# Routing as a pipeline over four batches, the last batch's row scatters moved into the expert block, and tile fields read eight at a time

## The chip, the core and the metric

The kernel runs on one core of a Trainium2 chip. The metric is the device time of one execution in microseconds (us); the engines are TensorE (PE), VectorE (DVE), ScalarE (ACT), GpSimd (POOL) and SyncE (SP). SP and POOL issue the DMAs.

## What is computed

The input is `x` (4 batches of 512 tokens with 512 channels) and a context. Four residual steps follow one another: a cross attention, a feed-forward layer whose weights come from spline control points, a selective scan, and a mixture of experts. Only the last two steps touch the change:

```python
x = x + _L1_xattn_ref(ctx_1024, _layernorm(x), ...)      # y * silu(z), z = layernorm(x)
x = x + _L1_ffn_ref(_layernorm(x), gate_kernel, gate_proj, up_proj, down_proj)

router_logits = x2d @ gate_kernel                        # 2048 tokens, 32 experts
routing_weights, selected = top_k(softmax(router_logits), 8)
routing_weights = routing_weights / sum(routing_weights)
inter = silu(rows_of_expert @ gate_proj[e]) * (rows_of_expert @ up_proj[e])   # 512 -> 192
output[token] += routing_weight * (inter @ down_proj[e])                      # 192 -> 512
```

## The kernel before, in words

The program is a row of blocks; at the end of a block every engine waits for all others. Blocks A and B (attention, feed-forward, scan) end at about 1055 us of the trace and are not touched.

**Block C** (`block_c`, L750) finishes the scan step and routes. It goes over the four batches one after the other; a batch is 4 tiles of 128 tokens. For each batch DVE normalizes `z` (L390), ACT takes its silu (L958), DVE multiplies with `y` (L854), PE turns the product (L976), DVE adds it to `X` (L858) and takes the statistics of the new `X` (L862 to L872), writes the normalized rows into `C_row` (L876), PE turns them (L981), ACT copies them (L963) and PE makes the router's logits (L986, 16 small matmuls, two records each). DVE then does softmax and top 8 (L882 to L900), PE counts the places of the rows in each expert's region (L991 to L995), and DVE writes the 32 destination rows of each partition into `C_where` (L909). POOL then issues 32 scatters (L829), one for each tile and each of a token's 8 experts; each writes 128 rows of 2180 bytes (512 channels, 32 weights, the token's number) into `rows_d` in HBM. Two row buffers alternate. After the fourth batch DVE computes 168 entries of tile fields in the tensor `meta` (L933 to L951): for each tile of 128 rows its expert, its first row, its weight slot and flags. SP appends to each of the 32 experts' regions a tile of padding (L810 to L813), and waits for all of them before the block ends.

**Block D** (`block_d`, L1007) computes the experts. SP loads the weights of experts 0 and 1 (L1045, L1046) and the first 8 row tiles (L1051), ACT and POOL split the weights in high and low parts (L1142, L1143; L1197, L1198). A loop then takes 8 tiles in one turn (`UNROLL`). For each tile PE turns the inner product of the tile (L1114), does gate and up of the next tile (12 matmuls, `split_products`, L1087 to L1089), turns the rows of the tile after that (L1083) and does the down product (6 matmuls). DVE copies the result (L1192) and POOL adds it into the output with an indirect DMA (L1218). SP refills the row buffer once the tile's addition has landed (L1070, L1071). At each expert's first tile SP loads the weights of the expert three further on, ACT and POOL split those of the expert two further on.

The engines read a tile's fields with `field` (L1036), one `value_load` of one word: PE three for each tile (its slot, the next slot, the next expert), ACT one flag for each tile and three more where it splits, POOL two flags and three more, SP one flag and a base, and two more where it loads weights.

Of the kernel before, what the change touches and what calls it, by code (L numbers as in the profile page):

```python
# [39 lines left out]
ROW = D + NE + 1  # L40
REGION = NB * L + P
# [52 lines left out]
def build(nc, a):  # L94
# [9 lines left out]
    with ctx:  # L104
# [12 lines left out]
        block_c(nc, a, X, ident, bank, meta, y0_d, y1_d, rows_d)  # L117
        block_d(nc, a, ident, bank, meta, rows_d)
# [631 lines left out]
def block_c(nc, a, X, ident, bank, meta, y0_d, y1_d, rows_d):  # L750

    with ExitStack() as s:
        sb, sem = mem(nc, s, "C")
        st, mv, rstd = sb("st", [P, NT, 6]), sb("mv", [P, NT, 2]), sb("rstd", [P, NT])
        st2, mv2, rstd2 = sb("st2", [P, LT, 6]), sb("mv2", [P, LT, 2]), sb("rstd2", [P, LT])
        y = [sb(f"y{i}", [P, LT, L]) for i in range(2)]
        z, yg = sb("z", [P, LT, D]), sb("yg", [P, LT, L])  # L760
        gk, hT = sb("gk", [P, KC, NE]), sb("hT", [P, LT, D])
        row = [sb(f"row{i}", [P, LT, ROW]) for i in range(2)]
        tok = sb("tok", [P, NT], I32)
        before, ones = sb("before", [P, P]), sb("ones", [P, P])
        lg, ex, pr, rest, chosen, place = (sb(n, [P, LT, NE]) for n in ("logit", "expo", "prob", "rest", "chosen", "place"))
        mx, sm, inv, tsum, tinv = (sb(n, [P, LT]) for n in ("mx", "sm", "inv", "tsum", "tinv"))
        top, top_place = sb("top", [P, LT, TOPK]), sb("top_place", [P, LT, TOPK])
        where = [sb(f"where{i}", [P, LT, TOPK], I32) for i in range(2)]
        fill = sb("fill", [P, NE])
        pad = sb("pad", [P, ROW])  # L770
        incl, neg_base, tau, tau0 = sb("incl", [NE, NE]), sb("neg_base", [NE, 1]), sb("tau", [NE, NMETA]), sb("tau0", [1, NMETA])
        need_i, need_s, need, ends = sb("need_i", [NE, 1], I32), sb("need_s", [NE, 1], I32), sb("need", [NE, 1]), sb("ends", [NE, 1])
        past = sb("past", [NE, NMETA])
        ev, sc, dd, f0, f1 = (sb(n, [1, NMETA]) for n in ("ev", "sc", "dd", "f0", "f1"))
        i0, i1 = sb("i0", [1, NMETA], I32), sb("i1", [1, NMETA], I32)
        padrow = sb("padrow", [1, NE], I32)

        stats, root, ln_step, ln_var, ln_rooted = sem("stats"), sem("root"), sem("ln_step"), sem("ln_var"), sem("ln_rooted")
        ld_y, joined, ld_c = [sem(f"ld_y{i}") for i in range(2)], [sem(f"joined{i}") for i in range(2)], sem("ld_c")
        z_in, z_done, g_done, yT_ps, x2_done, h_in, h_ps, h_sb, lg_ps = (sem(n) for n in ("z_in", "z_done", "g_done", "yT_ps", "x2_done", "h_in", "h_ps", "h_sb", "lg_ps"))  # L780
        passed = sem("passed")
        r_step, r_in, r_exp, chosen_done, rank_ps, where_done, scattered, fill_done = (
            sem(n) for n in ("r_step", "r_in", "r_exp", "chosen_done", "rank_ps", "where_done", "scattered", "fill_done"))
        fT_ps, need_done, ends_ps, past_done, meta_ps, m_step, padrow_done, stored = (
            sem(n) for n in ("fT_ps", "need_done", "ends_ps", "past_done", "meta_ps", "m_step", "padrow_done", "stored"))
        block = s.enter_context(nc.Block())
        RS = 15
        out = a["out"]
        consts = ((gk[:, :, :], "gk"), (tok[:, :], "tok"), (before[:, :], "before"), (ones[:, :], "ones"), (fill[:, :], "fill"),
                  (pad[:, 0:ROW - 1], "pad"), (pad[:, ROW - 1:ROW].bitcast(I32), "pad_tok"), (incl[:, :], "incl"),  # L790
                  (neg_base[:, :], "neg_base"), (tau[:, :], "tau"), (tau0[:, :], "tau0"))

        @block.sync
        def _(sp):
            for b in range(2):
                sp.dma_start(y[b][:, :, :], y0_d[b]).then_inc(ld_y[b], 16)
            for dst, name in consts:
                sp.dma_start(dst, a[name]).then_inc(ld_c, 16)
            sp.wait_ge(ld_c, 16 * len(consts))

            sp.dma_start(rows_d[NE * REGION:NE * REGION + P, :], pad[:, :]).then_inc(stored, 16)
            sp.dma_start(out[NT * P:NT * P + P, :], pad[:, 0:D]).then_inc(stored, 16)
            for b in range(NB):
                if b + 2 < NB:
                    sp.wait_ge(g_done, b + 1)
                    sp.dma_start(y[b % 2][:, :, :], y0_d[b + 2]).then_inc(ld_y[b % 2], 16)
                sp.wait_ge(x2_done, 4 * b + 4)
                sp.dma_start(out[b * L:(b + 1) * L, :].rearrange("(t p) n -> p t n", p=P), X[:, b * LT:(b + 1) * LT, :]).then_inc(stored, 16)
# [5 lines left out]
            sp.wait_ge(stored, 16 * (2 + NB + NE))  # L814

        @block.gpsimd
        def _(g):
            def join(b):

                g.wait_ge(ld_y[b % 2], 16 * (b // 2) + 16)  # L820
                g.dma_start(y[b % 2][:, :, :], y1_d[b], accum_op=ALU.add).then_inc(joined[b % 2], 16)

            join(0)
            join(1)
            for b in range(NB):
                g.wait_ge(where_done, b + 1)
                for t in range(LT):
                    for k in range(TOPK):
                        g.indirect_dma_start(rows_d[:, :], bass.IndirectOffsetOnAxis(ap=where[b % 2][:, t, k:k + 1].bitcast(U32), axis=0),  # L829
                                             row[b % 2][:, t, :], None).then_inc(scattered, 16)  # L830
                if b + 2 < NB:
                    join(b + 2)
                g.wait_ge(scattered, (b + 1) * 16 * LT * TOPK)

        @block.vector
        def _(v):
            ln_statistics(v, X, st, mv, rstd, stats, root, 0)
            v.wait_ge(ld_c, 16 * len(consts))
# [4 lines left out]
            def batch(base, h):  # L843
                def step(i, n):
                    i.then_inc(r_step, 1)
                    v.wait_ge(r_step, base * RS + n)
                    if n in (4, 5, 13):
                        v.sem_inc(passed)
                for t in range(LT):
                    i = ln_tile(v, X, base * LT + t, mv, rstd, z[:, t, :])  # L850
                i.then_inc(z_in, 1)
                v.wait_ge(z_done, base + 1)
                v.wait_ge(joined[h], pair * 16 + 16)
                v.tensor_tensor(yg[:, :, :], y[h][:, :, :], z[:, :, :], ALU.mult).then_inc(g_done, 1)  # L854
                for t in range(LT):
                    v.wait_ge(yT_ps, base * 4 + t + 1)
                    x = X[:, ds(base * LT + t, 1), :].rearrange("p o n -> p (o n)")
                    v.tensor_tensor(x, bank[t][:, :], x, ALU.add).then_inc(x2_done, 1)  # L858
                v.wait_ge(x2_done, base * 4 + 4)
                v.sem_inc(passed)  # L860
                for t in range(LT):
                    i = v.bn_stats(st2[:, t, :], X[:, ds(base * LT + t, 1), :])  # L862
                i.then_inc(ln_step, 1)
                v.wait_ge(ln_step, base * 3 + 1)
                v.sem_inc(passed)
                for t in range(LT):
                    i = v.bn_aggr(mv2[:, t, :], st2[:, t, :])
                i.then_inc(ln_step, 1)
                v.wait_ge(ln_step, base * 3 + 2)
                v.tensor_scalar(rstd2[:, :], mv2[:, :, 1], EPS, None, ALU.add).then_inc(ln_var, 1)  # L870
                v.wait_ge(ln_rooted, base + 1)
                v.reciprocal(rstd2[:, :], rstd2[:, :]).then_inc(ln_step, 1)  # L872
                v.wait_ge(ln_step, base * 3 + 3)
                v.wait_ge(scattered, pair * ((1 + h) * 16 * LT * TOPK))
                for t in range(LT):
                    v.tensor_scalar(row[h][:, t, 0:D], X[:, ds(base * LT + t, 1), :].rearrange("p o n -> p (o n)"), mv2[:, t, 0:1],  # L876
                                    rstd2[:, t:t + 1], ALU.subtract, ALU.mult).then_inc(h_in, 1)
                v.tensor_copy(row[h][:, :, ROW - 1:ROW].bitcast(I32), tok[:, ds(base * LT, LT)].rearrange("p (t o) -> p t o", o=1))

# [9 lines left out]
                for t in range(LT):  # L889
                    i = v.max(top[:, t, :], pr[:, t, :])  # L890
# [22 lines left out]
            with v.Fori(0, NB // 2) as pair:  # L913
                for h in range(2):
                    batch(pair * 2 + h, h)
# [361 lines left out]
```

## Time and profile before

| what | value |
|---|---|
| median of 3 runs | 2109.48 us (2105.89 to 2111.84) |
| profiled execution, its own time | 2110.38 us |
| its span, first to last instruction | 2108.6 us |
| busy share of the span | PE 78%, DVE 51%, ACT 36%, POOL 58% |
| block C | 1055 to 1339 us |
| block D | 1339 us to the end, 144 tiles |

The span is the time from the first to the last recorded instruction. Busy time counts work of the engines' data paths only; reading a register from memory, a branch or a wait is not busy time, and shows as "issue" where nothing else explains that an engine stood idle. Where a row says "remote", the engine was released by an event that no record of this core explains.

### The profile page before, as it was taken

What the parts mean: (1) busy time and instruction counts of PE and PEld (TensorE: products, weight loads), DVE (VectorE), ACT (ScalarE), POOL (GpSimd) and SP (SyncE); (2) the same over time, 40 slices, a digit from 0 to 9 for tenths busy, and PEclk for the clock granted to TensorE, in tenths of its full rate; (3) what the DMA queues carried; (4) which work ended last, traced back from release to release, by engine and by line L of the source; (5) the groups of instructions that cost most, each with busy time, mean ns of one, the idle gap of its engine ahead of it and who ended that gap; (6) DMA issues with size and microseconds to landing.
All of it is one profiled execution on the core that took longest, in us unless ns stands there. A gap on an engine that the chain in (4) does not pass through costs nothing. (4 is left out here: it accounts for less than half of the span.)

```text
span 2108.6 us, 28900 instructions
## 1 busy us (share of the span) xinstructions
PE 1643.6 (78%) x6083; PEld 1036.1 (49%) x6084; DVE 1070.7 (51%) x1770; ACT 762.8 (36%) x1072; POOL 1225.3 (58%) x552
## 2 busy tenths in 40 slices
PE   5887577989899999999933221299888998988886
PEld 2333233444344444444433221277777777777775
DVE  3566665555656565656552331054554544544453
ACT  3434345555555555555421110132222322232221
POOL 0111239888888888889715665256555545655552
PEclk9888779999999999999955555599999999999998
DMA  3111325668576767767656647667777877877776
GB/s 110 71 70 71 149 93 147 146 129 194 125 140 153 166 130 140 164 132 138 120 156 214 209 189 252 218 123 163 159 162 151 161 146 165 168 160 161 146 141 114
DMA packets 100442, 313.48 MB, mean 149 GB/s; under 512 B 13633, under 2 KB 14562, under 8 KB 88530
## 3 DMA queue, kind: packets, MB, share of 16 engines
q0 software_dynamic: 40896, 144.79, 35.9%
q1 hardware_dynamic: 59410, 167.42, 26.5%
q14 instruction: 117, 0.96, 0.2%
q8 instruction: 19, 0.31, 0.1%
HBM read 145.08 MB, written 167.08 MB: 148 GB/s over the span
## 5 line engine op out<-in xcount | busy, mean ns | idle before, releaser
L684 DVE TENSOR_TENSOR_SCAN B_E<-bank,B_E 128x512 f32<-128x512 f32 x256 | 306.4, 1212 | 206.7 <-ACT bank L639 199.2
L1218 POOL DMA_INDIRECT out_x<-D_y,D_rows x144 | 223.0, 1549 | 293.2 <-issue 177.8
L727 POOL TENSOR_TENSOR B_E<-B_E,B_Cb 128x2048 f32<-128x2048 f32 x64 | 291.8, 4559 | 110.9 <-DVE B_E L684 110.9
L721 POOL TENSOR_TENSOR B_E<-B_dtu,B_Bb 128x2048 f32<-128x2048 f32 x64 | 292.1, 4565 | 33.2 <-DMA B_Bb<-bc_d 33.2
L600 PE MATMUL bank<-B_Wd,B_inter 128*128 128x512 f32 x512 | 230.7, 596 | 33.2 <-DVE X L678 32.4
L590 PE MATMUL bank<-hT,B_Wg 128*128 128x512 f32 x512 | 236.8, 606 | 23.5 <-DVE B_inter L673 22.4
L590 PE MATMUL bank<-hT,B_Wu 128*128 128x512 f32 x512 | 230.2, 592 | 0.0
L1087 PE MATMUL bank<-D_gu_hi,D_xT_hi 128*128 x580 | 215.1, 371 | 15.5 <-DVE D_xT_lo L1176 8.3
L639 ACT ACTIVATE bank<-B_dtv,negA 128x512 f32<-128x512 f32 x256 | 171.8, 687 | 137.8 <-DVE B_E L684 137.0
L1171 DVE SCALAR_TENSOR_TENSOR D_inner<-D_sil,D_rows,bank 128x192 f32<-128x192 f32 x145 | 60.1, 414 | 308.4 <-ACT D_sil L1139 300.0
L1139 ACT ACTIVATE D_sil<-bank 128x192 f32<-128x192 f32 x145 | 47.2, 326 | 427.8 <-PE bank L1089 424.4
L1089 PE MATMUL bank<-D_gu_hi,D_xT_lo 128*128 x580 | 200.3, 345 | 0.0
L1088 PE MATMUL bank<-D_gu_lo,D_xT_hi 128*128 x580 | 200.0, 345 | 0.0
L829 POOL DMA_INDIRECT rows_d<-C_row,C_where x128 | 129.7, 1013 | 118.1 <-DVE C_where L909 80.3
L600 PEld LDWEIGHTS bank<-B_Wd,B_inter 128*128 128x128 f32 x512 | 92.7, 189 | 155.7 <-issue 92.0
L590 PEld LDWEIGHTS bank<-hT,B_Wg 128*128 128x128 f32 x512 | 97.3, 194 | 144.6 <-issue 142.8
L1197 POOL TENSOR_TENSOR D_gu_lo<-D_raw_gu,D_gu_hi (+1 forms) x32 | 111.2, 3474 | 81.9 <-issue 41.9
L590 PEld LDWEIGHTS bank<-hT,B_Wu 128*128 128x128 f32 x512 | 97.3, 190 | 122.5 <-issue 122.5
L1176 DVE TENSOR_TENSOR D_xT_lo<-bank,D_xT_hi 128x512 fp32r<-128x512 f32 x146 | 101.0, 692 | 88.9 <-ACT D_xT_hi L1135 88.0
L1083 PE MATMUL bank<-ident,D_rows 128*128 128x128 f32 x584 | 89.9, 277 | 71.4 <-DMA D_rows<-rows_d 71.4
L1087 PEld LDWEIGHTS bank<-D_gu_hi,D_xT_hi 128*128 128x128 f32 x580 | 112.8, 194 | 43.5 <-issue 36.9
L1087 PE MATMUL bank<-D_d_hi,D_iT_hi 96*128 x288 | 125.9, 437 | 0.0
(205 smaller groups left out, 2713.1 us busy)
## 6 DMA issues: line engine op xcount, KB each, us to landing
y_d<-B_E POOLq DMA_DIRECT2D x64, 1024.0 KB, 8.0
D_rows<-rows_d SPq DMA_DIRECT2D x152, 272.5 KB
D_raw_gu<-in_wgu SPq DMA_DIRECT2D x32, 768.0 KB
B_Bb<-bc_d SPq DMA_DIRECT2D x32, 512.0 KB, 5.4
B_Cb<-bc_d SPq DMA_DIRECT2D x32, 512.0 KB, 4.0
D_raw_d<-in_wd SPq DMA_DIRECT2D x32, 384.0 KB
rows_d<-C_pad SPq DMA_DIRECT2D x33, 272.5 KB
X<-in_x SPq DMA_DIRECT2D x4, 1024.0 KB, 9.1
```

Source lines behind the costliest of these rows:

```text
L590: mm = pe.matmul(ps[:, :], W[:, k, ch * P:(ch + 1) * P], hT[:, k, tb * L:(tb + 1) * L], start=k == 0, stop=k == KC - 1)
L600: mm = pe.matmul(Yb[t % 2][:, :], inter[jj % 2][:, ch, t * P:(t + 1) * P], Wd[w][:, ch, :], start=ch == 0, stop=ch == 1)
L639: act.activation(dA[m % 2][:, :], dtv[:, c, :], ACT.Exp, scale=negA[:, c, n:n + 1]).then_inc(dA_done, 1)
L684: v.tensor_tensor_scan(E[:, s % NR, c, :], dA[m % 2][:, :], E[:, s % NR, c, :], 0.0, ALU.mult, ALU.add).then_inc(s_done, 1)
L721: g.tensor_tensor(E[:, s % NR, :, :], dtu[b % 2][:, :, :], spread(Bb[jj % 2][:, s % 2, :]), ALU.mult).then_inc(dbu_done, 1)
L727: g.tensor_tensor(E[:, s % NR, :, :], E[:, s % NR, :, :], spread(Cb[jj % 2][:, s % 2, :]), ALU.mult).then_inc(prod_done, 1)
L829: g.indirect_dma_start(rows_d[:, :], bass.IndirectOffsetOnAxis(ap=where[b % 2][:, t, k:k + 1].bitcast(U32), axis=0), row[b % 2][:, t, :], ...
L1087: pe.matmul(ps, hi, whi, start=n == 0, stop=False)
L1088: pe.matmul(ps, hi, wlo, start=False, stop=False)
L1089: return pe.matmul(ps, lo, whi, start=False, stop=last)
L1197: g.tensor_tensor(slot(gu_lo, buf), slot(raw_gu, raw), slot(gu_hi, buf), ALU.subtract)
L1218: g.indirect_dma_start(a["out"], bass.IndirectOffsetOnAxis(ap=rows[i][:, ROW - 1:ROW].bitcast(U32), axis=0), ysb[i][:, :], None, compute_o ...
```

## The change

- `X` normalization and silu become one ACT activation for each tile, with a scale and a shift (`silu`); the rows are normalized by ACT too (`rows`). DVE keeps the statistics, additions and routing.
- The batches are interleaved: each engine has an order written out by hand (`gate`, `residual`, `normal`, `route`, `choose`, `rank` on DVE). There is a row buffer for every batch, so no batch waits for the scatters of another. The ranks come from 2 matmuls of 128 columns for each batch instead of 14 of 32.
- The weights of experts 0 and 1 are loaded and split in block C (class `Weights`), in POOL's queue ahead of the first scatter.
- Block C scatters batches 0 to 2 only and pads experts 0 to 15. Block D begins with the 32 scatters of batch 3, the lowest of each token's experts first; SP loads row tile `i` when the scatters of the first `i + 1` places have landed, then the weights of expert 2, then pads experts 16 to 31, waits for these, and enters the loop.
- In the loop PE reads nine slots and nine experts in one `load` each at the head of 8 tiles, and ACT its eight split flags; the ring positions are computed from the expert's number instead of being read.
- The result tiles use the space of `X`.

```diff
-FIELDS = 11
-BASE, EXPERT, SLOT, FIRST, LOADS, SPLITS, LOAD_RAW, SPLIT_RAW, SPLIT_SLOT, GO, RLOADS = range(FIELDS)
+FIELDS = 8
+BASE, EXPERT, SLOT, FIRST, LOADS, SPLITS, GO, RLOADS = range(FIELDS)
# block C, POOL
+            join(2)
+            join(3)
+            split(0)
+            split(1)
+            for b in range(NB - 1):
+                scatter(b)
# block C, DVE
+            gate(0)
+            gate(1)
+            residual(0)
+            residual(1)
+            gate(2)
+            normal(0)
+            residual(2)
+            normal(1)
+            v.wait_ge(ld_c, 16 * len(consts))
+            route(0)
+            gate(3)
+            choose(0)
+            residual(3)
+            normal(2)
+            rank(0)
+            route(1)
+            choose(1)
+            normal(3)
+            rank(1)
...
# block C, ACT
+            def silu(b):
+                if b >= 2:
+                    act.wait_ge(yT_ps, 4 * (b - 1))
+                for t in range(LT):
+                    q = LT * b + t
+                    act.activation(z[b % 2][:, t, :], X[:, q, :], ACT.Silu, bias=shift[:, q:q + 1], scale=rstd[:, q:q + 1]).then_inc(z_done, 1)
...
+            split(0)
+            sqrt(2)
+            expo(0)
+            rows(1)
+            hidden(1)
+            sqrt(3)
+            split(1)
...
# block C, SP
-            for e in range(NE):
-                first = sp.value_load(padrow[0:1, e:e + 1], min_val=e * REGION, max_val=(e + 1) * REGION - P)
-                sp.dma_start(rows_d[ds(first, P), :], pad[:, :]).then_inc(stored, 16)
+            for e in range(PADS_FIRST):
+                W.pad(sp, e, rows_d, pad, padrow).then_inc(stored, 16)
# block D
+        def fields(eng, regs, f, tile, hi):
+
+            eng.load(regs, meta[0:1, f, ds(tile, len(regs))])
+            return [eng.snap(r, min_val=0, max_val=hi) for r in regs]
# block D, SP
+            sp.wait_ge(scattered, 16 * (NT - LT) * TOPK)
             for i in range(UNROLL):
                 first = field(sp, BASE, i, NE * REGION)
+                sp.wait_ge(late[TOPK - 1 - i], 16 * LT)
                 sp.dma_start(rows[i][:, :], rows_d[ds(first, P), :]).then_inc(ld_rows[i], 16)
+            W.load(sp, 2, 0)
+            for e in range(PADS_FIRST, NE):
+                W.pad(sp, e, rows_d, pad, padrow).then_inc(padded, 16)
+            sp.wait_ge(padded, 16 * (NE - PADS_FIRST))
# block D, PE
+                    bufs = fields(pe, slots, SLOT, q * UNROLL, NSLOT - 1)
+                    of = fields(pe, experts, EXPERT, q * UNROLL, NE - 1)
                     for i in range(UNROLL):
                         t = q * UNROLL + i
-                        buf, next_buf = field(pe, SLOT, t, NSLOT - 1), field(pe, SLOT, t + 1, NSLOT - 1)
-                        next_expert = field(pe, EXPERT, t + 1, NE - 1)
# block D, POOL
+            for k in reversed(range(TOPK)):
+                for t in range(LT):
+                    g.indirect_dma_start(rows_d[:, :], bass.IndirectOffsetOnAxis(ap=where[:, NT - LT + t, k:k + 1].bitcast(U32), axis=0),
+                                         rows_last[:, t, :], None).then_inc(late[k], 16)
```

## Rows read from the trace of the kernel before

**Rows 1.** Windows over both blocks: stretch, length, busy of each engine, clock, DMA share.
```profile
1055.00:1101.00 46.00, 17.09 (x92) 16.42 (x92) 27.98 (x85) 11.44 (x13) 1.76 (x2) 0.58 0.54 161
1101.00:1159.00 58.00, 20.20 (x92) 19.53 (x92) 18.14 (x59) 8.66 (x10) 33.59 (x33) 0.50 0.63 209
1273.00:1339.00 66.00, 1.93 (x7) 0.60 (x7) 7.79 (x30) 0.00 (x0) 31.09 (x32) 0.50 0.78 271
1395.00:2109.00 714.00, 625.76 (x3297) 525.12 (x3295) 350.43 (x688) 191.25 (x334) 383.93 (x197) 0.97 0.75 154
```

**Rows 2.** Timeline of DVE in block C: start, length, line, idle before.
```profile
1071.45 2.29 DVE L854 TENSOR_TENSOR C_yg<-C_y,C_z 128x2048 f32<-128x2048 f32 x1 [2.08 <-ACT C_z L958]
1074.94 0.69 DVE L858 TENSOR_TENSOR X<-bank,X 128x512 f32 x1 [1.20 <-PE bank L976]
1082.15 1.92 DVE L876 TENSOR_SCALAR C_row<-X,C_mv,C_rstd 128x512 f32 x4
1090.03 0.29 DVE L882 TENSOR_REDUCE C_mx<-bank 128x4 f32<-128x128 f32 x1 [5.88 <-PE bank L986]
1101.30 0.18 DVE L909 TENSOR_SCALAR C_where<-C_top_place 128x32 int32<-128x32 f32 x1
1147.44 0.29 DVE L882 TENSOR_REDUCE C_mx<-bank 128x4 f32<-128x128 f32 x1 [28.60 <-remote]
```

**Rows 3.** POOL in block C: the scatters in 1150 to 1500 us grouped, then its timeline.
```profile
L829 POOL DMA_INDIRECT rows_d<-C_row,C_where x96 | 97.1, 1012 | 71.3 <-DVE C_where L909 43.0 <-issue 28.3
...
1159.69 1.01 POOL L829 DMA_INDIRECT rows_d<-C_row,C_where  x1 [14.86 <-DVE C_where L909]
1313.26 0.97 POOL L829 DMA_INDIRECT rows_d<-C_row,C_where  x1 [0.30 <-issue]
```

**Rows 4.** Timeline of PE in block C, second batch: the logits.
```profile
1120.77 6.88 PE L986 MATMUL bank<-C_gk,C_hT 128*128 128x32 f32 x32
```

**Rows 5.** Timeline of SP's queue: the padding during the scatters, and after them.
```profile
1274.49 39.23 SPq L813 DMA_DIRECT2D rows_d<-C_pad  x15
...
1318.62 17.49 SPq L813 DMA_DIRECT2D rows_d<-C_pad  x17
```

**Rows 6.** Timeline of PE at the start of block D: turned rows of tiles 0 and 8, first product.
```profile
1345.78 1.12 PE L1083 MATMUL bank<-ident,D_rows 128*128 128x128 f32 x4 [69.30 <-DMA D_rows<-rows_d]
1353.44 0.68 PE L1087 MATMUL bank<-D_gu_hi,D_xT_hi 128*128 x1 [6.55 <-POOL D_d_lo L1198]
1394.71 0.60 PE L1083 MATMUL bank<-ident,D_rows 128*128 128x128 f32 x4
```

**Rows 7.** Timelines of SP's queue and POOL, start of block D.
```profile
1340.54 8.07 SPq L1051 DMA_DIRECT2D D_rows<-rows_d  x8
...
1347.59 3.41 POOL L1197 TENSOR_TENSOR D_gu_lo<-D_raw_gu,D_gu_hi 128x1536 fp32r<-128x1536 f32 x1 [33.36 <-ACT D_d_hi L1143]
1350.97 2.33 POOL L1198 TENSOR_TENSOR D_d_lo<-D_raw_d,D_d_hi 96x1024 fp32r<-96x1024 f32 x1
```

**Rows 8.** DMA issues in 1055 to 1101 us: size and median time to landing.
```profile
C_y<-y_d POOLq DMA_DIRECT2D x2, 1024.0 KB, 11.6
```

**Rows 9.** Groups of PE in 1395 to 2109 us: busy, mean ns, idle before and its releaser.
```profile
L1087 PE MATMUL bank<-D_gu_hi,D_xT_hi 128*128 x556 | 205.0, 369 | 8.2 <-DVE D_xT_lo L1176 7.5 <-issue 0.4
L1114 PE MATMUL bank<-ident,D_inner 128*96 128x128 f32 x278 | 57.3, 288 | 60.1 <-issue 41.8 <-DVE D_inner L1171 17.6
```

**Rows 10.** Timeline of PE at the head of one turn of 8 tiles.
```profile
1524.26 0.42 PE L1114 MATMUL bank<-ident,D_inner 128*96 128x128 f32 x2 [1.57 <-issue]
```

**Rows 11.** Chain of waits in 1890 to 1900 us: POOL reads one field after another.
```profile
1896.53 0.29 POOLq L1036
...
1897.22 0.29 POOLq L1036
```

**Rows 12.** POOL: its additions on the page, and its waits for results in 1450 to 2030 us.
```profile
L1218 POOL DMA_INDIRECT out_x<-D_y,D_rows x144 | 223.0, 1549 | 293.2 <-issue 177.8
...
POOL out_x L1218 <- DVE D_y L1192: 42.2, 9, 7.3
```

More of the change, by code:

```diff
@@ L40 @@
 ROW = D + NE + 1
+GUW, MH = 2 * M, M // 2
+PADS_FIRST = NE // 2
 REGION = NB * L + P
@@ new lines, in _ @@
+            i.then_inc(stats, 1)
+            v.wait_ge(stats, 1)
+            for t in range(NT):
+                i = v.bn_aggr(mv[:, t, :], st[:, t, :])
+            i.then_inc(stats, 1)
+            v.wait_ge(stats, 2)
+            v.tensor_scalar(rstd[:, :], mv[:, :, 1], EPS, None, ALU.add).then_inc(stats, 1)
+            v.wait_ge(root, 1)
+            v.reciprocal(rstd[:, :], rstd[:, :]).then_inc(stats, 1)
+            v.wait_ge(stats, 4)
+            v.scalar_tensor_tensor(out=shift[:, :], in0=mv[:, :, 0], scalar=-1.0, in1=rstd[:, :], op0=ALU.mult, op1=ALU.mult).then_inc(shifted, 1)
@@ L906, in batch @@
                 for t in range(LT):
                     i = v.max(top_place[:, t, :], place[:, t, :])
-                step(i, 14)
-                v.tensor_scalar(where[h][:, :, :], top_place[:, :, :], -1.0, None, ALU.add).then_inc(where_done, 1)
-                step(v.tensor_tensor(fill[:, :], bank[2][:, 0:NE], fill[:, :], ALU.add), 15)
-                v.sem_inc(fill_done)
-            with v.Fori(0, NB // 2) as pair:
-                for h in range(2):
-                    batch(pair * 2 + h, h)
@@ new lines, in _ @@
+            route(0)
[8 more added lines that the diff above has]
+            rank(1)
+            route(2)
+            choose(2)
+            rank(2)
+            route(3)
+            choose(3)
+            rank(3)
+            v.tensor_scalar(padrow[:, :], fills[0:1, NT, :], -1.0, None, ALU.add).then_inc(padrow_done, 1)
+            step(v.tensor_tensor(count[:, :], fills[:, NT, :], fills[:, 0, :], ALU.subtract))
@@ new lines, in logits @@
+            def logits(b):
+                for t in range(LT):
+                    pe.wait_ge(row_done, LT * b + t + 1)
+                    if LT * b + t >= 2:
+                        pe.wait_ge(h_sb, LT * b + t - 1)
+                    for k in range(KC):
+                        mm = pe.transpose(bank[4 + t % 2][:, k * P:(k + 1) * P], row[b][:, t, k * P:(k + 1) * P], ident[:, :])
+                    mm.then_inc(h_ps, 1)
+                if b >= 2:
+                    pe.wait_ge(f_step, 5 * (b - 1))
+                for t in range(LT):
+                    pe.wait_ge(h_sb, LT * b + t + 1)
+                    for k in range(KC):
+                        mm = pe.matmul(bank[6 + b % 2][:, t * NE:(t + 1) * NE], hT[t // 2][:, t % 2, k * P:(k + 1) * P], gk[:, k, :], start=k == 0, stop=k == KC - 1)
+                mm.then_inc(lg_ps, 1)
@@ new lines, in ranks @@
+            def ranks(b):
+                pe.wait_ge(chosen_done, b + 1)
+                rhs = chosen[:, LT * b:LT * b + LT, :].rearrange("p t e -> p (t e)")
+                pe.matmul(bank[6 + b % 2][:, P:2 * P], before[:, :], rhs, start=True, stop=True)
+                pe.matmul(bank[6 + b % 2][:, 2 * P:3 * P], ones[:, :], rhs, start=True, stop=True).then_inc(rank_ps, 1)
+            turn_y(0)
+            turn_y(1)
+            turn_y(2)
+            logits(0)
+            turn_y(3)
+            logits(1)
@@ new lines, in _ @@
+            ranks(0)
+            logits(2)
+            ranks(1)
+            logits(3)
+            ranks(2)
+            ranks(3)
+            pe.wait_ge(ends_done, 1)
+            pe.transpose(bank[0][0:NE, 0:P], ends[:, :], ident[:, :])
+            pe.transpose(bank[1][0:NE, 0:P], need[:, :], ident[:, :]).then_inc(endsT_ps, 1)
+            pe.wait_ge(past_done, 1)
+            pe.matmul(bank[2][0:1, 0:NMETA], ones[0:NE, 0:1], past, start=True, stop=True)
+            pe.matmul(bank[3][0:1, 0:NMETA], need_c[:, :], past, start=True, stop=True).then_inc(meta_ps, 1)
```

476 lines of the change are left out of this document (257 added, 219 removed).

## The prediction

> **What bounds the kernel now.** I read the windows over blocks C and D first, then the timelines of DVE, POOL and SP in C, then the groups and the timeline of PE in D.
>
> In block C (1055 to 1339 us) no engine is busy: in 1101 to 1159 us PE works 20 of 58 us, DVE 18, ACT 9, POOL 34, and DMA stands at 0.63 [rows 1]. The order of work bounds it. Batch 0 needs 46 us until its destinations are written at 1101.30 [rows 2]. Then POOL scatters, and a scatter costs 1.012 us and 0.30 us of issue, 1.31 us together, so 42 us for the 32 of a batch [rows 3]. The next batch should be ready in that time. It isn't: DVE waits 28.60 us for "remote" until 1147.44 [rows 2], and POOL, done at 1159.69 - 14.86 = 1144.83, idles 14.86 us until the next destinations come [rows 3]. PE's last logits matmul is recorded at 1127.65 [rows 4], 20 us before DVE is released, and the release comes 2.6 us after POOL falls silent. So while POOL streams scatters, word between engines comes late. SP shows the same: with scatters running 15 paddings take 39.23 us, 2.62 each; without them 17 take 17.49 us, 1.09 each (the last one without its gap) [rows 5]. The fourth batch's scatters end at 1314.23 [rows 3], the padding at 1336.11 [rows 5], and the expert block starts at 1339.
>
> Block D begins with 14 us of loading and splitting before PE's first product at 1353.44; rows of tile 8 are turned at 1394.71 [rows 6]. After that PE is the bound: in the 714 us from 1395 its clock is at 0.97, the high level, and it is busy 625.76 [rows 1]; its gaps are 60.1 us ahead of the inner transpose (41.8 of them "issue", 17.6 DVE) and 8.2 ahead of the first product [rows 9]. The issue gaps are PE's sequencer reading three fields for each tile.
>
> **Terms.** My clock is the start of tile 8's row transposes, 1394.71 in the old trace: it lies behind all that C and the start of D do, and the loop behind it is the same work. Blocks A and B are untouched.
>
> *Start of C to the first scatter.* POOL's first scatter now stands behind both weight splits, and the second waits for ACT's `split(1)`, which waits for `sqrt(3)`, so for `residual(3)`. DVE's queue up to there: its first `gate` can start as now, at 1071.45; four gates of 2.29 (9.2); four residuals of 6.6 (1074.94 to the reciprocal just ahead of 1082.15, less its 0.4 of waiting for the root; 26.4); one softmax and top 8, the stretch from 1090.03 to 1101.30 without 5 us of waiting for PE and 1.4 of ranks (4.9); small steps 0.8 [rows 2]. Sum 1112.7. The loads of `y` for batches 2 and 3 follow the gates, and their accumulating DMA takes 11.6 us [rows 8]; with expert weights in the same DMA engines I add 5 us: 1117.7. Then ACT's split, an estimate of 2.5 (POOL's pass over the same elements, 3.41 + 2.33, is its upper bound), and POOL's 5.7 [rows 7]: 1126. This is 25 us later than now. Below: 1118, if the joins are not late; above: 1140.
>
> *Scatters of batches 0 to 2.* 96 of 1.31 us = 126 us [rows 3], if POOL never starves. Routing of the other batches needs some 34 us of DVE (three times the 11.3 from 1090.03 to 1101.30 [rows 2]) behind the first scatter in good conditions; the scatters of batch 1 are due 42 us after it, of batch 2 at 84. Even with every step two times slower while POOL streams, it arrives in time. End 1252; the tile fields and 16 paddings (at 2.62 us, 42 us [rows 5]) lie beside it. Block D starts at 1254.5 against 1339. The moved DVE work on ACT (16 silus, 16 row tiles) is beside idle time: ACT works 11 of the first 46 us [rows 1]. Fewer rank matmuls cost nothing and save nothing on the path. Where this cover fails is the second rival.
>
> *Start of D.* The 32 scatters of batch 3 take 42 us, to 1296.5. Tile 0 could start after the first four, but PE's word comes late under the stream, so I count one tile of progress until 1296.5. Then PE needs 7 tiles of 4.6 us (625.76 busy over 136 tiles [rows 1]) to reach tile 8's rows: 1329. SP in the meantime: last row tile issued at 1298, weights of expert 2, 16 paddings at 1.09 = 17.5 us [rows 5] and 2 for landing: 1318; then three fields, the next weights, and the row load (4 us), which lands 5.2 us later, as the first did (1340.54 to 1345.78 [rows 6, 7]): 1327.5. Both come out alike; the later is 1329. So 1394.7 - 1329 = **66 us gained**. POOL starts its additions at 1297, some tiles late. It has slack: in 580 us of steady loop it waited 42.2 us for results [rows 12], and now reads two fields fewer at each split. The splits of expert 2 are due only at tile 9 or so (144 additions [rows 12] over 32 experts).
>
> *The loop.* One field read costs 0.69 us from read to read (1896.53 to 1897.22), 0.29 of it the read itself [rows 11]. PE drops three for each tile. What they hide behind are the six down products, so only the excess shows: 1.57 us at the head of a turn [rows 10], less at other tiles. After: at the 17 heads behind my clock two reads of nine words. From below they cost 2 x 0.69 = 1.4 us; from above 18 x 0.69 = 12.4. No row shows a read of more than one word. I take 3.6 us, near the lower end, because the 0.4 us around a read are address and bounds steps that one read needs once. The three old ones were 2.1, so the head's gap grows from about 1.5 to 3.0: 17 x 3.0 = 51. Of the other gaps (8.2 ahead of the product stays; of the 17.6 for DVE most were ACT's four reads ahead of a split, now one) 15 stay. Total 66 against 68.3 now [rows 9]; with ACT's help I say **5 us gained**. At the lower end 0.8 x 17 + 15 = 29, 40 us gained; at the upper end 11.8 x 17 + 15 = 216, 147 lost.
>
> The Trainium skill ("Runtime: NRT & Kernel Launch", the launch sequence) speaks against this part: a register load costs about 200 ns for each register, even in bulk. By it the 18 words are 3.6 us without what stands around them, and the sum would be some 20 us worse. The rows show 0.29 us for one word and no more.
>
> **Sum.** 2110.4 (the profiled execution, span 2108.6 and 1.8 around it) - 66 - 5 = 2039. The median is 0.9 below this execution: **2038 us**.
>
> **Rivals.**
> 1. *Reads are cheap and tiles overlap the last scatters.* For it: no row says that a further word is dear. Gain in the loop up to 40 instead of 5, and a few us earlier at tile 8: 2110 - 70 - 38 = 2002. Against: three out of three batches show late word under the stream.
> 2. *POOL starves in C.* If the late word holds up routing as now, POOL idles 15 us before each of batches 1 and 2 again [rows 3], and the first scatter may be at 1140: 2038 + 30 to + 44 = 2075. Against: all heavy PE work (the logits of batch 3) is queued before or near the first scatter.
> 3. *Slower than before: nine words cost nine reads.* Place: the head of each turn of 8 tiles on PE. Price: 18 x 0.69 = 12.4 us there, 147 us lost over the loop against 66 gained: 2190. It decides from the point where the 18 words cost 3.6 + 71/17 = 7.8 us, 0.43 us a word. For it: the read itself is 0.29 us; against: the rest of the 0.69 shouldn't repeat.
> 4. *The loop doesn't move at all*, since PE then waits for DVE and ACT: 2043. It is within the forecast's own range.
>
> The Trainium skill ("SBUF — State Buffer", who interferes with whom) says that TensorE and ScalarE never wait on anyone and only VectorE and GpSimd share a port. The 28.60 us and SP's 2.62 against 1.09 us don't fit this [rows 2, 5]. By the rule tiles would run beside the last scatters, and the sum would still be within 2 us, since the padding holds tile 8 until 1327.5.
>
> **Numbers.** Forecast with its own range 2015 to 2060: 0.50. Rival 1: 0.20. Rival 2: 0.15. Rival 3: 0.10. Others, such as the expert block slowed by POOL's late additions: 0.05. The range takes rival 1 and 2 in and leaves the worst of 3 out: 1988 to 2090. A change under 0.3% (6 us) can't be told from none here. Faster 0.88 (forecast, rivals 1 and 2, some of the rest), same 0.02, slower 0.10.
>
> **What would show it.** First scatter near 1126; no gap of POOL over 3 us between the 96 scatters; block D near 1255; row transposes of tile 8 near 1329, released by the row load; in the loop PE's gaps ahead of the inner transpose near 3 us at every eighth tile and small elsewhere. Wrong if the first scatter comes after 1140, if POOL waits for destinations again, or if the gap at the heads is over 8 us.

## The result, and the profile after

| | before | after |
|---|---|---|
| device time, median (range, runs) | 2108.67 us (2105.89 to 2111.84, 4) | 2031.14 us (2028.05 to 2034.64, 4) |
| ratio, 95% interval | | 0.9623 [0.9604, 0.9642] |
| profiled execution, its span | 2110.38, 2108.6 | 2028.05, 2026.0 |
| mean granted clock of PE | 0.894 | 0.902 |
| row transposes of tile 8 start | 1394.71 | 1364.39 |
| from there to the end of the span | 713.9 | 661.6 |

The kernel gained 77.5 us in the medians and 82.6 between the two profiled spans (the new kernel's profiled execution is the fastest of its four). The forecast said 2038, 71 us less: 66 ahead of tile 8 and 5 behind it. Measured are 30.3 ahead of it (1394.71 - 1364.39) and 52.3 behind it (713.9 - 661.6). The total is right for the wrong reasons: both terms are far off, in opposite directions.

The windows of the new kernel by stage (columns as in [rows 1]): from the start of C to the first scatter, the first 64 scatters, POOL's gap, the next 32, the barrier, the 32 late scatters, up to tile 8, and the loop.

```profile
1055.00:1133.00 78.00, 30.18 (x177) 27.47 (x178) 52.95 (x145) 43.19 (x58) 15.71 (x13) 0.60 0.66 202
1133.00:1214.00 81.00, 20.98 (x93) 19.71 (x91) 7.02 (x39) 6.48 (x11) 61.69 (x64) 0.50 0.57 217
1214.00:1226.00 12.00, 0.00 (x0) 0.00 (x0) 2.49 (x13) 0.17 (x1) 0.44 (x1) 0.50 0.06 23
1226.00:1266.00 40.00, 3.11 (x10) 1.38 (x10) 11.69 (x57) 0.14 (x1) 30.32 (x32) 0.50 0.70 265
1266.00:1282.00 16.00, 0.00 (x0) 0.00 (x0) 0.00 (x0) 0.00 (x0) 0.06 (x1) 0.50 0.46 174
1282.00:1322.00 40.00, 12.57 (x44) 10.78 (x44) 2.64 (x5) 2.81 (x4) 30.55 (x32) 0.59 0.74 258
1322.00:1364.00 42.00, 29.96 (x134) 25.70 (x134) 14.98 (x30) 7.65 (x14) 17.43 (x13) 0.78 0.82 228
1364.00:2026.00 662.00, 613.30 (x3298) 528.42 (x3298) 351.68 (x688) 198.35 (x334) 383.87 (x196) 0.98 0.76 165
```

In two stretches that the forecast didn't have hardly any engine works, 28 us together: 12 us in the middle of the scatters and 16 us at the end of block C. POOL's waits in C and at the start of D name them (line, what it waited for, us in total, times, longest); in the old kernel it waited 43.0 us for destinations between the batches [rows 3].

```profile
POOL rows_d L851 <- issue: 28.8, 95, 0.3
POOL rows_d L1363 <- POOLq L760: 16.2, 1, 16.2
POOL rows_d L851 <- DVE where L964: 11.6, 1, 11.6
```

The late word of [rows 2] ("word" is the news, by a semaphore, that another engine is done) is back in another place. On PE's timeline the last rank product of batch 2, the third, is recorded at 1167.64; on DVE's the addition that waits for it starts at 1223.04, 9 us after POOL's last scatter of that stream ended (1213.01 + 0.96).

```profile
1167.64 0.37 PE L1124 MATMUL bank<-C_chosen,C_ones 128*128 128x128 f32 x1 [1.03 <-issue]
```

```profile
1223.04 0.87 DVE L957 TENSOR_TENSOR C_fills<-bank,C_fills 128x32 f32<-128x32 f32 x4 [74.52 <-remote]
```

```profile
1213.01 0.96 POOL L851 DMA_INDIRECT rows_d<-C_row,where  x1 [0.30 <-issue]
1225.56 0.96 POOL L851 DMA_INDIRECT rows_d<-C_row,where  x1 [11.59 <-DVE where L964]
```

SP's queue in the new kernel: the first 16 paddings take 44.74 us, 2.8 each on average. That average mixes two rates: the first seven, beside scatters, cost 5.1 us each (1233.89 to 1269.71), the last eight, behind them, 1.09. The 8 row loads take 37.65 us beside the late scatters (8.07 without, [rows 7]).

```profile
1233.89 44.74 SPq L1168 DMA_DIRECT2D rows_d<-pad  x16
1288.84 37.65 SPq L1215 DMA_DIRECT2D D_rows<-rows_d  x8
```

In the loop (PE's waits from 1364 on) two kinds are left; the waits for DVE, 17.6 and 7.5 us in [rows 9], are gone.

```profile
PE bank L1278 <- issue: 32.9, 17, 2.7
PE bank L1246 <- DMA D_rows<-rows_d: 4.1, 1, 4.1
```

The most telling line is a small one in the page's table of DMA queues, which nobody would read first: packets, MB and share of the instruction queue q14 (its packets bring parts of an engine's program), before and then after.

```profile
q14 instruction: 117, 0.96, 0.2%
```

```profile
q14 instruction: 29, 0.24, 0.0%
```

The old kernel loads 88 packets of 8 KB more. In the 16 turns from 1403.56 to 2053.89 there are 80, 5 a turn; the new kernel has none between 1374 and 2027 us.

### The profile page after: what moved, and what is told of

Same layout as the page of the kernel before. It is cut to its first block and busy times, and to the rows that moved or that the text cites. A ratio compares the mean times of both kernels' runs of the same rounds, so it can differ in the third digit from the quotient of the medians.

```text
span 2026.0 us, 26118 instructions
## 1 busy us (share of the span) xinstructions
PE 1612.5 (80%) x5986; PEld 1022.0 (50%) x5987; DVE 1058.9 (52%) x1748; ACT 779.3 (38%) x1097; POOL 1220.6 (60%) x557
## 5 line engine op out<-in xcount | busy, mean ns | idle before, releaser
L1380 POOL DMA_INDIRECT out_x<-X,D_rows x144 | 224.0, 1556 | 279.2 <-DVE X L1353 129.1
L608 PE MATMUL bank<-B_Wd,B_inter 128*128 128x512 f32 x512 | 230.7, 597 | 33.2 <-DVE X L686 32.4
L1250 PE MATMUL bank<-W_gu_hi,D_xT_hi 128*128 x580 | 216.3, 373 | 3.2 <-DVE D_xT_lo L1337 1.8
L1251 PE MATMUL bank<-W_gu_lo,D_xT_hi 128*128 x580 | 200.5, 346 | 0.0
L1252 PE MATMUL bank<-W_gu_hi,D_xT_lo 128*128 x580 | 200.1, 345 | 0.0
L1250 PEld LDWEIGHTS bank<-W_gu_hi,D_xT_hi 128*128 128x128 f32 x580 | 112.9, 195 | 35.3 <-issue 33.5
L1250 PE MATMUL bank<-W_d_hi,D_iT_hi 96*128 x288 | 127.2, 442 | 0.0
L366 POOL TENSOR_SCALAR A_one<-A_ex 128x2048 f32<-128x2048 f32 x4 | 21.5, 5368 | 169.6 <-ACT A_ex L281 169.6
L1299 ACT ACTIVATE D_xT_hi<-bank 128x512 fp32r<-128x512 f32 x146 | 87.1, 597 | 85.5 <-issue 67.6
```

Of the source, the lines that this page charges most:

```text
L608: mm = pe.matmul(Yb[t % 2][:, :], inter[jj % 2][:, ch, t * P:(t + 1) * P], Wd[w][:, ch, :], start=ch == 0, stop=ch == 1)
L1250: pe.matmul(ps, hi, whi, start=n == 0, stop=False)
L1251: pe.matmul(ps, hi, wlo, start=False, stop=False)
L1252: return pe.matmul(ps, lo, whi, start=False, stop=last)
L1380: g.indirect_dma_start(a["out"], bass.IndirectOffsetOnAxis(ap=rows[i][:, ROW - 1:ROW].bitcast(U32), axis=0), ysb[i], None, compute_op=ALU. ...
```

## Experiments

The diffs show the lines that matter; registers, names and helpers that go with them are left out.

Times are medians of the runs made beside the kernel before on the same chip (its medians there: 2114.5 us for the first four kernels, 2113.3 for the last four), so ratios are compared between the two groups and times within one. "Tile 8" is the start of that tile's row transposes; "loop" is the time from there to the last tile's inner transposes in the profiled execution: 691.4 us before, 641.8 after. Three kernels leave the loop's work as it is in the new one (pe_waits16, last_in_c24, pause8). With the new kernel's, their loops span 641.8 to 647.3 us, and the time that PE's clock stands at 0.50 in them goes with it: 13.7, 17.1, 27.3 and 27.3 us. So a difference of less than 6 us between two loops isn't clear by itself.

| kernel | time | ratio, 95% | loop | q14 packets |
|---|---|---|---|---|
| pe_waits16 | 2031.8 | 0.9606 [0.9575, 0.9638] | 642.4 | 29 |
| new_pe_three_reads | 2039.1 | 0.9637 [0.9605, 0.9669] | 654.6 | 29 |
| new_act_single_flags | 2035.9 | 0.9639 [0.9600, 0.9678] | 645.5 | 29 |
| old_pe_nine_words | 2115.5 | 1.0004 [0.9988, 1.0020] | 688.5 | 117 |
| new_pool_long | 2066.0 | 0.9781 [0.9753, 0.9809] | 672.0 | 117 |
| old_pool_short | 2100.0 | 0.9949 [0.9932, 0.9967] | 680.9 | 29 |
| last_in_c24 | 2038.0 | 0.9649 [0.9616, 0.9682] | 645.2 | 29 |
| pause8 | 2043.6 | 0.9671 [0.9643, 0.9699] | 647.3 | 30 |

### Is it PE's program that is fetched again?

**pe_waits16**

```diff
+                        pe.wait_ge(W.hi_done, 1)
+                        pe.wait_ge(xT_first, 1)
```

> The new kernel with 16 waits more in each turn of 8 tiles on PE (two behind every tile's first-layer products, on semaphores that were passed long ago). They read nothing and stand where PE has 12 products queued. In the trace PE issues 511 instructions in a turn of the new kernel and 595 in one of the old; the old one loads some 8 packets of 8 KB of instructions a turn, the new one none between 1373 and 2027 us. Theory A (the loop gained because PE's turn no longer has to be fetched again): 511 + 16 instructions are over the limit again, the packets are back and the kernel takes 2051 to 2076 us. Theory B (the loop gained because PE reads fewer fields): the waits are hidden, 2031 +- 6 us, no packets.

Measured: 2031.8 us, loop 642.4 (641.8 without the waits), 29 packets. Theory A in this form falls: that PE's turn is 511 instructions with the gain and 595 without it was a coincidence. (The old kernel's packets are 5 a turn, not the 8 of the text above.)

**new_pe_three_reads** (the edit is the old code of PE, in the new kernel)

```diff
-                    bufs = fields(pe, slots, SLOT, q * UNROLL, NSLOT - 1)
-                    of = fields(pe, experts, EXPERT, q * UNROLL, NE - 1)
+                        buf, next_buf = field(pe, SLOT, t, NSLOT - 1), field(pe, SLOT, t + 1, NSLOT - 1)
+                        next_expert = field(pe, EXPERT, t + 1, NE - 1)
```

> The new kernel with PE reading its three fields one by one at every tile, as the old kernel did; everything else is new. Theory A (instruction fetching): PE's turn is near 595 instructions again, packets are back, and the loop loses all of its gain, 45 us or so: 2076. Theory B (the reads' own time): the gaps put down to issue go from 33 to 41 us and the waits for VectorE stay away: 2040.

Measured: 2039.1 us. Its runs (2037.5 to 2043.3) lie above all of pe_waits16 (2027.3 to 2032.9) on the same chip, 7 us apart; the loop of the profiled execution is 12.8 us longer. PE's waits there:

```profile
PE bank L1277 <- issue: 35.2, 43, 2.1
```

Theory B named the time, 2040 us, and that no wait for DVE comes back, but not the gaps: it said 41 us, and there are 43 short waits of 35.2 us for 16 of 32.4 in the same stretch. Many small gaps for a few large ones is nearly an even trade in waiting. Most of the 12.8 us lies in PE's busy time, 621.0 us behind tile 8 for 613.3, with the clock at 0.50 for 23.9 us of it, not 13.7. This profiled execution is also the slowest of its four and the new kernel's the fastest, so 12.8 is more than the 7 us of the medians.

**old_pe_nine_words**

```diff
-                        buf, next_buf = field(pe, SLOT, t, NSLOT - 1), field(pe, SLOT, t + 1, NSLOT - 1)
-                        next_expert = field(pe, EXPERT, t + 1, NE - 1)
+                    bufs = fields(pe, slots, SLOT, q * UNROLL, NSLOT - 1)
+                    of = fields(pe, experts, EXPERT, q * UNROLL, NE - 1)
```

> The old kernel with one change: PE reads nine slots and nine experts at the head of a turn, as the new one does. ScalarE, GpSimd and SyncE read as before, block C is the old one. Theory A (instruction fetching): the whole gain of the loop comes from this, 2109 - 45 = 2064 us, no instruction packets in the steady loop. Theory B (the reads' own time, the rest of the gain from ScalarE's fewer reads): 2109 - 8 = 2101 us.

Measured: no change (1.0004). Both theories miss, A by some 45 us, B by 9. The very edit that looked like the point of the new loop is worth nothing in the old one, because something else held PE up there. Its waits show the shift: the issue gaps fall from 41.3 (in this view) to 34.0 us, the waits for DVE rise from 17.6 to 20.6 and from 7.5 to 9.6, and waits for rows from 2.2 to 4.0.

```profile
PE bank L1124 <- issue: 34.0, 19, 2.8
PE bank L1124 <- DVE D_inner L1181: 20.6, 23, 2.7
PE bank L1096 <- DVE D_xT_lo L1186: 9.6, 24, 0.5
```

**new_act_single_flags**

```diff
-                        with act.If(to_split[i] > 0):
+                        with act.If(field(act, SPLITS, t, 1) > 0):
```

> The new kernel with ScalarE reading its split flag one by one at every tile as before (8 reads a turn for one of eight words). Theory A (PE's instructions alone): no change, 2031 +- 6 us. The rival (the waits of PE for VectorE, 25 us in the old loop, came from ScalarE's reads): up to 25 us more, 2056.

Measured: 2035.9 us, 4 more than pe_waits16 on the same chip (2034.7 to 2045.2 against 2027.3 to 2032.9), the loop 3.7 longer, which alone would not be clear. Its waits are: 5.2 us of waiting for DVE's `xT_lo` are back, and none of the kernels with an unchanged loop has any. ScalarE's flags are a small part.

### Is it POOL's?

**new_pool_long**

```diff
                             split_lo(ring(g, e, SPLIT_AHEAD, NRAW), ring(g, e, SPLIT_AHEAD, NSLOT))
+                            for _ in range(8):
+                                g.wait_ge(W.hi_done, 1)
+                                g.sem_inc(passed)
```

> The new kernel with POOL's loop made longer, not slower: eight passed waits, each with a count, behind every weight split, inside the branch that only every fourth tile or so takes (some 2 a turn). Written out, a turn of POOL is then 337 instructions; it is 273 in the new kernel and 313 in the old. The theory that PE's program was being fetched again fell with the first runs: 16 instructions more on PE brought no packet, nine-word reads in the old kernel took none away, and all kernels on the new base have none, all on the old base 83. Of the 85 packets in the old loop 43 land just ahead of the first addition of a turn on POOL. Theory A (POOL's loop is what is fetched): the 8 KB packets come back in the steady loop and it is as slow as the old one, 30 to 45 us more, 2061 to 2076. Theory B (fetching is a by-product, or is another engine's): none or few packets, 2031 +- 6 us.

Measured: ratio 0.9781 against 0.9623 of the new kernel, the intervals far apart: 0.0158 x 2108.7 = 33 us slower. The packets are back, as many as on the old kernel's page, and the loop is 30.2 us longer. The page's line and then POOL's waits in 1420 to 2000 us of this kernel:

```profile
q14 instruction: 117, 0.96, 0.2%
```

```profile
POOL out_x L1380 <- issue: 171.4, 95, 8.7
POOL out_x L1380 <- DVE X L1353: 40.1, 12, 6.8
```

The same waits in the new kernel:

```profile
POOL out_x L1380 <- DVE X L1353: 107.2, 38, 6.6
POOL out_x L1380 <- issue: 102.0, 79, 6.6
```

In the new kernel POOL waits mostly for results: it has slack. With the longer program 69 us more are "issue", its own sequencer, and it waits for results only 12 times. It runs late; row buffers then come free late, and PE gets waits that it didn't have (its waits from 1395 us on):

```profile
PE bank L1246 <- DMA D_rows<-rows_d: 9.6, 7, 3.5
PE bank L1278 <- DVE D_inner L1332: 7.6, 6, 1.8
```

All PE's waits there are 49.1 us for 32.4, so they make up 17 of the 30 us. The other 13 are PE's busy time behind tile 8, 626.61 us for 613.30. The clock stands at 0.50 for 37.5 us of the loop, not 13.7, in 11 falls for 4; at the 1.3 us that a fall costs below, some 9 us of the 13 (an estimate).

```profile
1365.00:2063.00 698.00, 626.61 (x3298) 537.37 (x3298) 350.79 (x688) 196.06 (x334) 383.69 (x196) 0.96 0.73 157
```

The added waits take 0.69 us at each of 30 splits, 21 us in all, on an engine that waits 107 us for results; that alone is not the 69 us. The records of POOL's sequencer show where the rest is. Behind the branch that ends a turn its next record comes after 3.9 us, behind the one that begins the next after 2.2 (medians), 111 us over the loop, a part of it while a split or an addition still works. In the new kernel the same two steps take 0.19 and 0.13 us.

**old_pool_short**

```diff
-                            raw, buf = field(g, SPLIT_RAW, t, NRAW - 1), field(g, SPLIT_SLOT, t, NSLOT - 1)
+                            raw, buf = ring(g, e, SPLIT_AHEAD, NRAW), ring(g, e, SPLIT_AHEAD, NSLOT)
```

> The old kernel with one change, on POOL alone: the two buffer numbers of a split are worked out from the expert (an addition and a mask each) and no longer read. Written out, POOL's turn falls from 313 to 273 instructions, the new kernel's number. Theory A (POOL's loop was fetched again each turn and that slowed the others): the packets go and the old loop gains 30 to 45 us, 2064 to 2079. Theory B (the time of the reads): 30 splits times two reads of 0.69 us on an engine with slack, 2109 +- 6.

Measured: 0.9949 [0.9932, 0.9967], 11 us faster, and the 88 packets are gone. Two reads less, in a branch taken twice a turn, do this. Behind the branch that ends a turn POOL's sequencer stood still for 4.5 us in the old kernel (median of 16, 3.4 to 8.0, 78 us together); here it is 0.20 us. So POOL's program is what was fetched, shown from both sides. But the 30 to 45 us were not there: PE then still reads three fields a tile, and keeps 33.5 us of issue gaps and 26.4 us of waits for DVE. How the 11 us divide between the fetching and the reads that POOL no longer does (30 times two of 0.69 us, 41 us) is not separated. POOL waited 52.6 us for results in 1420 to 2000 us before, and waits 111.3 now.

### The scatters

**last_in_c24**

```diff
-PADS_FIRST = NE // 2
+PADS_FIRST = 24
-            for b in range(NB - 1):
+            for b in range(NB):
                 scatter(b)
```

> The new kernel with the last batch's 32 scatters back in block C, in token order, and 24 paddings (for 16) ahead of block D. Theory M (moving the scatters into the expert block pays, since tiles start beside them): putting them back costs about what is taken away, tile 8 some 15 us later, 2046. Theory N (it doesn't pay: SP's row loads and paddings, slow beside the scatters, set tile 8 at 1364): scatters end at 1306, the barrier waits for nothing else, 8 row loads take 8 us, PE starts at 1316 and reaches tile 8's rows after 8 tiles of 4.6 us at 1353 to 1356, 8 to 11 us earlier than now: 2021.

Measured: 0.9649 [0.9616, 0.9682], some 5 us slower than the new kernel with intervals that overlap; tile 8 at 1372.11. Neither theory's number. Theory N failed on the paddings: SP's queue shows 24 of them at 3.86 us each on average, up to 1327.3, 17 us behind the last scatter (1309.51 + 0.96). (The 32 late scatters of block D, and the waits for them, are left out of this kernel.)

```profile
1234.56 92.74 SPq L1168 DMA_DIRECT2D rows_d<-pad  x24
1330.53 8.46 SPq L1214 DMA_DIRECT2D D_rows<-rows_d  x8
```

From its first row transposes (1333.40) this kernel reaches tile 8 in 38.7 us. The new kernel needs 71.8 (1292.63 to 1364.39), since its first tiles stand beside the late scatters. What the late scatters are worth without the paddings in the way was not measured.

**pause8**

```diff
                                              row[b][:, t, :], None).then_inc(scattered, 16)
+                    g.wait_ge(scattered, 16 * TOPK * (LT * b + t + 1))
```

> The new kernel with POOL waiting in block C after every 8 scatters until they have landed (12 pauses, some 3 us each). In the new kernel word from PE that is due at 1168 us reaches DVE at 1223, 9 us after the stream of 64 scatters stops, and SP takes 0.7 us for every instruction from 9 us after the next stream starts until its end. Theory P (something piles up while POOL scatters without a break, and a pause of 3 us clears it): DVE's wait ahead of the third batch's ranks falls from 74 us to under 15, no wait of POOL for destinations, a padding on SP costs 1.1 to 1.5 us for 2.8, and the barrier no longer waits for it: 36 us lost in pauses against 11.6 + 16 gained, so 2031 to 2043. Theory Q (the pauses are too short or it is no pile): the same late word and 30 us more, 2061.

Measured: 2043.6 us, at theory P's upper end. Its signs of early word hold; that something piles up isn't shown by them (see Open). DVE's longest wait for ranks is 9.5 us and PE's record ends it; all routing is done at 1176 us (in the new kernel at 1241); 16 paddings take 1.35 us each. DVE's waits, SP's queue, and POOL's waits of this kernel:

```profile
DVE C_fills L958 <- PE bank L1125: 16.8, 2, 9.5
```

```profile
1167.96 21.67 SPq L1169 DMA_DIRECT2D rows_d<-pad  x16
```

```profile
POOL rows_d L851 <- DMA rows_d<-C_row,where: 28.5, 11, 5.2
POOL rows_d L851 <- issue: 25.8, 85, 0.3
POOL rows_d L1364 <- POOLq L760: 11.2, 1, 11.2
```

One part of P was wrong. The barrier at the end of C still costs 11.2 us, though the paddings were done at 1189.6 and the last scatter had landed. The trace holds an instruction DRAIN of POOL there, 8.21 us long. In the new kernel POOL's drain ends 8.2 us behind its last scatter's end (in last_in_c24 only 2.5), so of its 16.2 us at the barrier half is the drain and only the other half is SP's late paddings. 28.5 us of pauses bought 11.6 and some 5: a loss, with nine of the twelve pauses behind 1176 us, where all routing was done.

## Why the prediction was right, and where it wasn't

The time came out right because a gain 36 us too small ahead of tile 8 met one 47 us too large behind it, and that is luck.

**Ahead of tile 8: 66 forecast, 30.3 measured.** Step by step, from forecast to measured, in us later than forecast:

| step | forecast | measured | later |
|---|---|---|---|
| first scatter | 1126 | 1133.08 | 7.1 |
| 96 scatters | 1.31 each | 1.265 each | -4.3 |
| POOL without destinations | 0 | 11.6 | 11.6 |
| last of the 96 to the first late one | 2.5 | 16.2 | 13.7 |
| 32 late scatters | 42 | 40.2 | -1.8 |
| from their end to tile 8 | 32.5 | 42.3 | 9.8 |

The sum is 36.1, and 1329 + 36.1 = 1365.1 for 1364.39 measured.

- *First scatter.* Inside its bounds. The queue of DVE was right in order; the chain over ACT's second split into POOL's was what released it, as said.
- *"If POOL never starves ... even with every step two times slower while POOL streams, it arrives in time."* This step failed. For DVE the late word isn't a slower rate: it is a stop until POOL falls silent, as 28.60 us in [rows 2] already said. The bound should have been: whatever is due some 20 scatters into the stream comes at its end (PE's products ended 26 us into it in the old kernel, 27 in the new one). Rival 2 had the mechanism and the place, but two gaps of 15 us; there was one of 11.6, because the ranks of batch 1 came 9 us into the stream, while word was still prompt, and everything for batches 2 and 3 passed in one gap. pause8 confirms that an unbroken stream is the condition.
- *Barrier.* The 16 paddings were set "beside" the scatters, 42 us long. They were, but they could start only at 1233.89 for the same late word. And the end of block C has a drain on POOL, to 8.2 us behind the scatters, that no term held. In the old kernel it was hidden: scatters end at 1314.23, the drain at 1324.37, paddings at 1336.11 [rows 5].
- *Start of D.* The late word was priced on PE ("one tile of progress") but not on SP: its last row load goes out at 1326 and not at 1298, and paddings, landing and weights follow from there. The order of work was right: tile 8 is released by its row load, as said, 4.14 us after PE was ready.

**The loop: 5 forecast, 52.3 measured.** Four things were wrong; in the first only the size. Of the 52.3 us, some 40 are idle time of PE and 12.5 busy time.

- *The reads.* 3.6 us for 18 words at the head. In the records of PE's sequencer the first list takes 1.17 us and the second 0.85 (medians of 18; 0.83 to 1.69), one word 0.31. With more cover than assumed the gap at a head is 32.9 / 17 = 1.94 us for the 3.0 forecast: 18 us of the miss. The Trainium skill ("Runtime: NRT & Kernel Launch", the launch sequence and instruction fetch mechanics) gives its 200 ns for each register for loads from HBM. The fields lie in SBUF, and the second list shows 94 ns a word, so the figure didn't bear on this term. Nor did it make the sum 20 us worse: by the prediction's own steps of 0.4 us around a read, two at each of 17 heads, it is 14.
- *"Of the other gaps 15 stay."* None stayed. [rows 9] names them as waits for DVE, and the forecast explained them by ACT's four reads. Giving ACT its single flags back brings 5.2 us of waiting and 4 us of time, and fetching on POOL 10.4 us of waiting. What took the rest of the 25 us away isn't shown. ACT executes 67 instructions a turn for 103 in the old kernel, 97 with its flags back.
- *Instruction fetching.* Not seen at all, although the page of the old kernel had its 117 packets in plain sight. Against the loop of the new kernel, POOL's longer program costs 30.2 us, PE's single reads 12.8, ACT's single flags 3.7. That is 46.7 of the 49.6 us between the two loops (691.4 - 641.8), but a sum of single executions that can each be off by some 5 us. From the old kernel's side the same parts are worth 10.5 (old_pool_short) and 3 (old_pe_nine_words). They don't add up from that side, so there the parts hide behind one another. No run takes two of them out of the old kernel at once, so which hides which isn't shown.
- *The clock.* No term held it. At 4 of the 17 heads the granted clock falls in the gap or just behind it, for 3.4 us, and the next tile takes 5.5 to 5.8 us, not 4.4: some 5 us in all. The old loop had 8 such falls, in more irregular gaps; so some 5 of the loop's 12.5 us less of busy time on PE (625.76 in [rows 1], 613.30 above) are these. Windows around one head of the new kernel:

```profile
1634.00:1636.00 2.00, 0.79 (x4) 0.31 (x2) 1.38 (x2) 1.39 (x2) 0.00 (x0) 1.00 1.07 143
1636.00:1638.00 2.00, 0.95 (x4) 0.88 (x5) 0.26 (x1) 1.07 (x2) 0.10 (x1) 0.64 0.35 127
1638.00:1640.00 2.00, 2.00 (x8) 2.00 (x7) 0.58 (x2) 0.00 (x0) 1.86 (x2) 0.50 0.49 140
1640.00:1642.00 2.00, 2.00 (x13) 1.84 (x13) 0.41 (x1) 0.93 (x2) 2.00 (x1) 1.00 1.13 174
```

PE stands idle for 2.25 us at 1634.8, and comes back at 0.50, which is 1.2 GHz: 8 products in 2 us, not 13. Gaps of 2.43 and 2.69 us at other heads passed without a fall.

**Rivals.** Rival 1's first half ("no row says that a further word is dear") is true of the reads, but cheap reads didn't make the loop's gain: alone in the old kernel they brought 3 us. Its second half (tiles overlap the last scatters) is not what happened: tile 8 came 35 us later than forecast. Rival 3 is out: 18 words are 2.0 us of reading, far from 7.8. Of the signs named, the late first scatter (1133 of at most 1140) and the gap at the heads (1.94 of at most 8) stayed within their marks; "wrong if POOL waits for destinations again" did come true, for one batch. The rule on shared ports that the prediction holds against the late word is one of access to SBUF. Word by semaphore isn't in it, so the 28.60 us neither bear it out nor break it.

**Open.** Why word stops while POOL scatters. In the new kernel SP's instructions, plain register moves too, come alone or in pairs at steps of some 0.7 us from 9 us into the second stream up to its end (0.06 to 0.4 us apart behind it), so it isn't semaphores alone. It isn't a pile of data: the last packet of a scatter ends 2.4 us after the scatter's record starts (median; at most 4.1), and for the last one ahead of the gap it is 2.4 too, at 1215.4, while the word comes at 1223.0. So the scatters' data don't run behind POOL's record either, though POOL's drain ends 8 to 10 us behind its last recorded scatter in all kernels but last_in_c24. What the streams do crowd out is semaphore news in the trace itself: of the 1536 increments by the first 96 scatters the new kernel's trace holds 252, that of pause8 1198. Which path is full, and whether the recording takes part in it, isn't shown. In the loop it is not separated whether POOL's program was fetched for its length or for where its pages begin. Four further versions have no result: two with four pauses, one with PE's second list read behind tile 7's products, and one with both.

## What to carry to other kernels

Look at the packets of the instruction queue before pricing a loop: if they recur each turn, some engine's written-out loop is being fetched, branches that are hardly taken included, and shortening it can be worth more than the instructions removed. Price parts that hide behind one another together, since undoing one of them from the slow side can show next to nothing (3 of 50 us here). Count what PE's gaps do to its clock as well: of the 30 us that fetching on POOL cost, 13 lay in PE's busy time. Where an engine issues indirect DMAs without a break, treat word to and from the others as coming at the end of the stream, not as coming slower, and put everything that they need for the next stretch before it, the barrier's drain included.

## What the runs showed of the hardware

- POOL's loop of the old kernel is fetched in 8 KB packets, 5 a turn, and its sequencer stands still for 4.5 us behind the branch that ends a turn. PE's program, with 595 instructions executed a turn, isn't fetched again: POOL's two reads less took all these packets away. The Trainium skill says that each engine but PE has room for 512 instructions, PE for 2048, and that a taken branch out of the two pages held forces a fetch ("Runtime: NRT & Kernel Launch", instruction fetch mechanics). The trace agrees on PE and on the branch. On the size it decides nothing: POOL executes 152 instructions of a turn written out as 313, which is under 512, but where the pages begin isn't known. The packets of this queue are 8 KB, half of the 16 KB named; those of the other instruction queue, q8, are 16 KB.
- A read of nine words costs 0.85 to 1.17 us, one of one word 0.31: a further word is 0.07 to 0.11 us.
- A stream of scatters stopped word from PE for 55 us (1168 to 1223), and pauses of 2 to 5 us after every eighth scatter took that away.
- Idle times of PE of 1.9 to 2.3 us were followed by 3.4 us at 1.2 GHz at 4 of 17 heads, and ones of 2.4 to 2.7 us at other heads were not.
